# A Mamba-style mixer on one core: cumulated decays loaded as repeated rows in place of TensorE's spreading

## What is computed

```python
proj = einsum('bld,pd->blp', layernorm(x), in_proj_w)      # gate 4096, hbc 6144, dt 64
xBC = silu(causal_conv(hbc, 4 taps))                       # x: 64 heads x 64; B, C: 8 groups x 128
dt_p = softplus(dt + dt_bias); A = -exp(A_log)
state = state * exp(dt_p * A) + dt_p * x * B               # per head, row by row
y = state @ C + x * D
out = (group_norm(y) * norm_weight * silu(gate)) @ out_proj_w
```

## Time and profile before

| | |
|---|---|
| runs | median 1298.97 us (1296.31 to 1299.89), 3 runs |
| profiled execution | 1300.67 us |
| its span, first to last instruction | 1298.9 us |
| TensorE busy | 1230.5 us, 95% |
| VectorE busy | 933.9 us, 72% |
| ScalarE busy | 702.5 us, 54% |
| GpSimd busy | 653.6 us, 50% |

### The profile page before, as it was taken

How to read it: one execution, slowest core, us unless ns; L and a number is a source line. 1 busy time by engine, 2 the same in 40 slices (tenths; PEclk the granted TensorE clock), 3 DMA queues, 4 the chain that set the end, 5 groups by cost and what they waited for, 6 DMA issues and landing times. The chain is left out here.

```text
span 1298.9 us, 22009 instructions
## 1 busy us (share of the span) xinstructions
PE 1230.5 (95%) x6680; PEld 968.9 (75%) x6690; DVE 933.9 (72%) x1735; ACT 702.5 (54%) x1056; POOL 653.6 (50%) x707
## 2 busy tenths in 40 slices
PE   5999999999999999999999999999679999889976
PEld 4777777787778778777778878777557777667754
DVE  5786778669667866966886696688567555479995
ACT  3676676567567666756766675665543333222210
POOL 5057546655655655565465556545653343433330
PEclk9999999999999999999999999999789999889996
DMA  5111021011102101110210110010103322211100
GB/s 178 46 50 34 2 67 34 19 34 49 33 1 66 33 17 33 50 32 1 66 32 17 33 58 24 5 34 2 41 17 115 97 90 83 93 49 48 45 16 25
DMA packets 44233, 57.52 MB, mean 44 GB/s; under 512 B 10117, under 2 KB 21159, under 8 KB 43929
## 3 DMA queue, kind: packets, MB, share of 16 engines
q1 hardware_dynamic: 44185, 56.92, 14.3%
HBM read 49.95 MB, written 6.96 MB: 44 GB/s over the span
## 5 line engine op out<-in xcount | busy, mean ns | idle before, releaser
L722 DVE SCALAR_TENSOR_TENSOR conv<-p_tile,conv_taps,conv 128x511 f32<-128x511 f32 x189 | 141.3, 748 | 51.4 <-ACT conv L583 36.4
L831 DVE TENSOR_TENSOR em<-em,p_gb 128x512 f32<-128x512 f32 x128 | 82.1, 683 | 69.6 <-ACT em L630 69.5
L527 POOL TENSOR_TENSOR squares<-squares 128x256 f32<-128x256 f32 x64 | 48.0, 750 | 132.5 <-ACT squares L656 132.5
L94 PE MATMUL p_tile<-xn_hi,wc_hi 128*128 128x512 f32 x252 | 110.8, 440 | 0.9 <-DVE halo L726 0.9
L656 ACT ACTIVATE squares<-y 128x512 f32<-128x512 f32 x64 | 40.4, 631 | 112.5 <-DVE y L867 111.5
L722 DVE SCALAR_TENSOR_TENSOR conv<-p_gate,conv_taps,conv 128x511 f32<-128x511 f32 (+2 forms) x90 | 67.0, 745 | 46.7 <-ACT conv L583 43.1
L94 PE MATMUL p_tile<-xn_lo,wc_hi 128*128 128x512 f32 x252 | 98.8, 392 | 0.0
L94 PE MATMUL p_d<-wr_hi,zt_hi 128*128 128x512 f32 x236 | 94.0, 398 | 1.5 <-ACT em L630 1.5
L94 PE MATMUL p_d<-wr_lo,zt_hi 128*128 128x512 f32 x236 | 93.1, 394 | 0.0
L495 POOL TENSOR_TENSOR x_w<-xs,head_g 128x512 f32<-128x512 f32 x56 | 58.4, 1043 | 68.7 <-ACT xs L624 63.6
L588 ACT ACTIVATE xbc<-conv 128x512 f32<-128x512 f32 x96 | 60.7, 632 | 59.7 <-DVE conv L730 37.4
(11 more groups left out here) (393 smaller groups left out, 3605.1 us busy)
## 6 DMA issues: line engine op xcount, KB each, us to landing
w_raw<-w SPq DMA_DIRECT2D x108, 256.0 KB, 2.7
q_words<-q SPq DMA_DIRECT2D x33, 256.0 KB, 2.7
h_ring<-h_lo_rows SPq DMA_DIRECT2D x6, 704.0 KB, 4.8
h_lo_rows<-h_rest SPq DMA_DIRECT2D x11, 256.0 KB, 2.1
x_res<-x SPq DMA_DIRECT2D x8, 256.0 KB, 4.1
out<-out_t SPq DMA_DIRECT2D x8, 256.0 KB, 2.0
h_lo_rows<-h_rest SPq DMA_DIRECT2D x11, 128.0 KB, 1.9
gate_second<-w SPq DMA_DIRECT2D x4, 256.0 KB, 5.0
```

The source lines that it names most:

```text
L94: pe.matmul(out, lhs(k)[0], rhs(k)[n], start=(start and k == 0 and n == 0), stop=False)
L722: ve.scalar_tensor_tensor(out=conv[:, s, sh:], in0=p[:, 0:HALF - sh], scalar=conv_w[:, bass.ds(g, 1), j, tap], in1=conv[:, s, sh:], op0=AL ...
L831: ve.tensor_tensor(m, m, gm.unsqueeze(1).broadcast_to([P, HG // 2, P]), ALU.mult)\
```

## The change

- TensorE's decay products go, with `d_lhs`, `d_rhs`, `head_rows`, `load_d` and the bf16 parts. cum and exp(cum) are written to DRAM in fp32 as rows (`cum_rows`, `e_cum_rows`).
- `load_cum` loads the row block of a chunk's 8 heads, 1024 numbers, into all 128 partitions of em (512 KB), two chunks ahead, after s_intra of the buffer's last reader. `load_e_cum` loads each head's row into its 64 channels of e_cum (two DMAs of 128 KB), one chunk ahead, after s_t. VectorE's product with e_cum waits for s_ecl.
- `decay_steps` on ScalarE: for each of 8 heads Relu(cum_s - cum_t), 128x128, in place, with a column of cum_tok as bias, one chunk ahead, before the wait for s_y. Then em = exp(-that). Entries with s > t become 1 and are masked by VectorE's product. The exp of e_cum leaves the chunk loop.
- TensorE's waits for s_e and s_d go; those for s_v, s_res and s_t stay or move.
- Prologue: ScalarE normalizes (`ln_norm`), VectorE makes -mean times rstd of one column; ScalarE and GpSimd split w_dt, GpSimd makes the mask. The conv tiles use the banks p_tile, p_d1, p_in, p_x, p_tile, p_d1; four of them and a gate tile come before the transposes of dt.

The diff, cut (declarations, renumbered waits and removed constants are left out):

```diff
...
+    FIRST_BANK = (p_tile, p_d1, p_in, p_x, p_tile, p_d1)
...
-        def load_d(g, c):
+        def load_cum(g, c):
             n = g * NC + c
-            lhs_row, rhs_row = at(sp, g * PART * HG), at(sp, g * PART)
-            wait(sp, s_d, n - 1)
-            cs = slice(c * P, (c + 1) * P)
-            sp.dma_start(d_lhs[PART:PART + PART * HG, c % 2, :],
-                         parts.rearrange("g k h t -> (g k h) t")[bass.ds(lhs_row, PART * HG), cs])\
-                .then_inc(s_dl[c % 2], 16)
-            sp.dma_start(d_rhs[0:PART, c % 2, :].rearrange("k (h t) -> k h t", h=HG),
-                         parts.rearrange("g k h t -> (g k) h t")[bass.ds(rhs_row, PART), :, cs])\
-                .then_inc(s_dl[c % 2], 16)
+            wait(sp, s_intra, n - 1)
+            row = at(sp, g + c * G)
+            sp.dma_start(em[:, c % 2, :], cum_rows.rearrange("c (g h) t -> (c g) (h t)", g=G)[bass.ds(row, 1), :]
+                         .broadcast_to([P, HG * P])).then_inc(s_dl[c % 2], 16)
+        def load_e_cum(g, c):
+            wait(sp, s_t, g * (NC - 1) + c - 1)
+            row = at(sp, g + c * G)
+            own = e_rows.rearrange("c (g j a) t -> (c g) a j t", g=G, a=2)[bass.ds(row, 1)]
+            for a in range(2):
+                sp.dma_start(by_tile(e_cum[a * HD:(a + 1) * HD, :]),
+                             own[:, a, :, :].broadcast_to([HD, GW // P, P])).then_inc(s_ecl, 16)
...
-        for k in range(PART):
-            wait(sp, dt_ve, 12 + k)
+        for rows, made in ((cum_rows, (ln_st, NC + 3)), (e_rows, (dt_ac, 7))):
+            sp.wait_ge(*made)
             for a in range(2):
-                sp.dma_start(parts[:, k, :, a * HALF:(a + 1) * HALF], t_parts[k][a * H:(a + 1) * H, :])\
-                    .then_inc(s_parts, 16)
-        sp.wait_ge(s_parts, 16 * PART * 2)
-        sp.wait_ge(s_dconst, 80)
-        load_d(0, 0)
-        load_d(0, 1)
+                heads_a = (t_cum if rows is cum_rows else t_ecum)[a * H:(a + 1) * H, :]
+                sp.dma_start(rows[a * CH:(a + 1) * CH].rearrange("c h t -> h c t"),
+                             heads_a.rearrange("h (c t) -> h c t", t=P)).then_inc(s_parts, 16)
+        sp.wait_ge(s_parts, 16 * 4)
+        load_cum(0, 0)
+        sp.wait_ge(dt_tp, 4)
+        sp.wait_ge(dt_ve, 9)
+        load_cum(0, 1)
...
+                if c + 1 < NC:
+                    load_e_cum(g, c + 1)
                 if c + 2 < NC:
-                    load_d(g, c + 2)
+                    load_cum(g, c + 2)
                 elif not last:
-                    load_d(g + 1, c + 2 - NC)
+                    load_cum(g + 1, c + 2 - NC)
...
+        pool.memset(t_mask, 1.0).then_inc(s_split_dt, 1)
+        pool.wait_ge(s_split_dt, 1)
+        pool.memset(t_mask[:, 0:HALF:P], 0.0).then_inc(s_split_dt, 1)
...
+        pool.wait_ge(dt_ac, 1)
+        pool.tensor_tensor(lo_of(WT - 1), w_dt[:], hi_of(WT - 1).bitcast(F32), ALU.subtract).then_inc(s_split_dt, 1)
...
+        def decay_steps(g, c):
+            act.wait_ge(s_dl[c % 2], 16 * (g * (NC // 2) + c // 2 + 1))
+            for h in range(HG):
+                steps = em[:, c % 2, h * P:(h + 1) * P]
+                made = act.activation(steps, steps, ACT.Relu, scale=-1.0, bias=cum_tok[:, c, bass.ds(g * HG + h, 1)])
+            made.then_inc(s_e, 1)
...
-                act.wait_ge(s_d, n + 1)
-                wait(act, s_intra, n - 1)
-                if last and c >= CH:
-                    act.activation(e_cum[:], p_in[:], ACT.Exp).then_inc(s_ec, 1)
-                for k, p in enumerate((p_d0, p_d1)):
-                    act.activation(em[:, c % 2, k * 512:(k + 1) * 512], p[:], ACT.Exp).then_inc(s_e, 1)
-                if c > 0 and not (last and c >= CH):
-                    act.activation(e_cum[:], p_in[:], ACT.Exp).then_inc(s_ec, 1)
+                act.wait_ge(s_e, 3 * n + 1)
+                for k in range(2):
+                    decay = em[:, c % 2, k * 512:(k + 1) * 512]
+                    act.activation(decay, decay, ACT.Exp, scale=-1.0).then_inc(s_e, 1)
...
+                if c < NC - 1:
+                    decay_steps(g, c + 1)
+                elif not last:
+                    decay_steps(g + 1, 0)
...
+        def ln_norm(c):
+            act.wait_ge(ln_var, 3 * c + 3)
+            wait(act, ln_tr, c - 1)
+            act.activation(xnt[:, c % 2, :], x_res[:, c, :], ACT.Identity, bias=mean_var[:, c, 0:1],
+                           scale=rstd[:, c:c + 1]).then_inc(ln_xn, 1)
...
+        for c in range(NC + 1):
+            if c < NC:
+                ln_norm(c)
+            if c > 0:
+                ln_round(c - 1)
+            if c == CH:
+                act.wait_ge(s_const, 16 * 6)
+                act.activation(hi_of(WT - 1), w_dt[:], ACT.Copy).then_inc(dt_ac, 1)
+            if c > CH:
+                w_round(0, c - CH - 1)
...
+        tile_in(0, 0, 0, FIRST_BANK[0])
...
             tile_silu(j, 0, j, 0)
+            if j + 2 < TILES:
+                tile_in(j + 2, 0, j + 2, FIRST_BANK[j + 2])
             if j == 0:
+                gate_silu(0, 0, 0)
+                act.wait_ge(ln_st, NC + 3)
+                act.activation(t_ecum, t_cum, ACT.Exp).then_inc(dt_ac, 1)
+                act.wait_ge(dt_tp, 3)
+                act.activation(by_half(dtw_t), transposed(p_gb), ACT.Exp).then_inc(dt_ac, 1)
+                act.wait_ge(dt_tp, 4)
+                act.activation(by_half(etot_t), transposed(p_gate), ACT.Exp).then_inc(dt_ac, 1)
+            if j == 3:
+                gate_silu(1, 1, 0, p_in)
+            if j == 4:
                 gate_silu(2, 2, 0, p_x)
-            if j + 2 < TILES:
-                tile_in(j + 2, 0, j + 2, (p_tile, p_d1)[j % 2])
         gate_silu(3, 3, 0)
+        act.wait_ge(dt_ve, 11)
+        decay_steps(0, 0)
...
-            if 2 <= c < NC + 2:
-                ve.wait_ge(ln_rs, c)
-                wait(ve, ln_tr, c - 3)
-                ve.tensor_scalar(xnt[:, c % 2, :], x_res[:, c - 2, :], mean_var[:, c - 2, 0:1],
-                                 rstd[:, c - 2:c - 1], ALU.subtract, ALU.mult).then_inc(ln_xn, 1)
+            if 1 <= c <= NC:
+                ve.wait_ge(ln_rs, c + 1)
+                ve.scalar_tensor_tensor(out=mean_var[:, c - 1, 0:1], in0=mean_var[:, c - 1, 0:1], scalar=-1.0,
+                                        in1=rstd[:, c - 1:c], op0=ALU.mult, op1=ALU.mult).then_inc(ln_var, 1)
...
+        tile_taps(0, 0, 0, 0, range(TAPS), FIRST_BANK[0])
...
-        tile_taps(0, 0, 0, 0, range(TAPS), p_tile)
+        tile_taps(1, 0, 1, 0, range(TAPS), FIRST_BANK[1])
         ve.wait_ge(dt_tp, 3)
         ve.tensor_copy(by_half(dt_t), transposed(p_y)).then_inc(dt_ve, 1)
-        for j in range(1, TILES):
-            tile_taps(j, 0, j, 0, range(TAPS), (p_tile, p_d1)[j % 2])
-        ve.wait_ge(dt_ac, 7)
-        ve.wait_ge(dt_ve, 15)
+        ve.tensor_copy(by_half(cum_tok), transposed(p_d0)).then_inc(dt_ve, 1)
+        for j in range(2, TILES):
+            tile_taps(j, 0, j, 0, range(TAPS), FIRST_BANK[j])
...
-                wait(pe, s_tap, TAPS * (j - 1))
+                wait(pe, s_tap, TAPS * (j - 3))
...
-                pe.wait_ge(s_e, 2 * (n + 1))
+                wait(pe, l2_lo, {2: 1}.get(k, 0))
...
-                pe.wait_ge(s_dl[c % 2], 32 * (g * (NC // 2) + c // 2 + 1))
-                if c > 0:
-                    wait(pe, s_t, g * (NC - 1) + c - 1)
-                    for j in range(GW // P):
-                        pe.matmul(p_in[:, j * P:(j + 1) * P], head_rows[:, j, :], d_lhs[:, c % 2, :],
-                                  start=True, stop=True)
-                wait(pe, s_e, 2 * n)
-                wait(pe, s_res, n - 2 if tail and c > CH else n - 1)
-                wait(pe, s_v, n - 1)
                 if first:
                     pe.wait_ge(s_tap, TILES * TAPS)
-                for k in rows_in(last, c - 1):
-                    pe.wait_ge(l2_lo, k + 1)
-                for k, p in enumerate((p_d0, p_d1)):
-                    mm = pe.matmul(p[:], d_lhs[:, c % 2, :], d_rhs[:, c % 2, k * 512:(k + 1) * 512],
-                                   start=True, stop=True)
-                mm.then_inc(s_d, 1)
...
-                    pe.wait_ge(s_e, 2 * (n + 1))
+                    wait(pe, s_v, n - 1)
...
-                    pe.wait_ge(s_ec, g * (NC - 1) + c)
+                    wait(pe, s_t, g * (NC - 1) + c - 1)
...
+        conv_tile(0, 0, 0, 0, FIRST_BANK[0])
+        pe.wait_ge(dt_ve, 2)
+        for j in range(1, CH):
+            conv_tile(j, 0, j, 0, FIRST_BANK[j])
         gate_product(0, 0, 0)
-        gate_product(0, 1, 0, p_in)
+        pe.wait_ge(dt_ve, 9)
+        for src, dst in ((t_dt, p_y), (t_rem, p_gb), (t_cum, p_d0)):
+            for b in range(CH):
+                mm = pe.transpose(dst[:, b * P:(b + 1) * P], src[:, b * P:(b + 1) * P], ident[:])
+            mm.then_inc(dt_tp, 1)
+        for j in range(CH, TILES):
+            conv_tile(j, 0, j, 0, FIRST_BANK[j])
+            if j == CH:
```

(14 more changed lines are left out.)

126 lines of the change are left out of this document (32 added, 94 removed).

## The result

The changed kernel takes 1276.23 us, median of runs between 1275.21 and 1276.79; the kernel before, timed beside it, 1297.72. The ratio is 0.983, 95% interval 0.981 to 0.985: 21.5 us faster, a gain, but about half of the 44 forecast. So of the 22.5 us that are missing in the medians 18.5 are missing in the traces too, and those have places.

The account below looks back on a forecast made before the run. TensorE, busy all of a group's round, was taken as the bound. Columns 37.7, less 3 of waits, plus prologue 5.5 and tail 4 made 44 us, so a median of 1255; range 1241 to 1276.

Parts of the forecast that it names:

- rivals 1 and 3: ScalarE takes over as the bound, 1270 to 1286, 17%; SyncE's order makes weights late in chunk 0, 1276, 5%.
- TensorE's columns: Decay products gone from the mixer's chunks: 0.67 us saved per chunk, 0.44 in chunk 0, 37.7 us in all.
- A wait of about 0.1 us: Next chunk's conv tile waits for the gate's Silu in p_tile, in four chunks of a group: 3 us lost.
- With eight register offsets on top I allow 4: ScalarE's eight Relu steps per chunk: 2.6 us taken, 0.31 apart, upper bound 4 us with register offsets.
- Hidden: In chunk 0 the Relu steps make Square and xs 2.4 us later, without TensorE waiting for x_w.
- Prologue: Before the mixer: dt products start 4 us sooner, 1.5 us of bank waits go; 5.5 us saved, bounds 1 and 8.
- Tail: Last group's chunks 5 to 7: waits for xn_lo and e_cum go, x_w late next; 4 us saved, bounds 0 and 12.3.
- Transfers: Each chunk's 512 KB row block lands in 4 us, bounds 2.7 and 7, and is hidden, as are the out weights.
- The second: The ends give more, prologue 8 and tail 12 us, with no loss: 57.7 us saved, 1241; 10%.
- fourth: Slower: the 128 copies of one row land late and the first Relu waits for s_dl; 1396, 4%.
- fifth: The change doesn't do what it says, as TensorE's columns were hidden; 1295, 3%.

Follow-up runs that it names:

- tuned: both, but in the last four chunks of the last group the product of C and the state keeps its old place; 1257.26 us, ratio 0.967.
- both: Changed kernel with the product of C and the state ahead of the conv tile and ScalarE's loop written out; 1258.47 us, ratio 0.967.
- wide_relu: tuned with a chunk's eight Relu steps made one of 128x1024 with a single bias column (decays not the reference's); 1251.95 us, ratio 0.963.
- inter_first: Changed kernel with TensorE's product of C and the state moved ahead of the same chunk's conv tile; 1266.67 us, ratio 0.976.
- scalar_unrolled: Changed kernel with ScalarE's loop over the six middle groups written out, other engines keeping theirs; 1268.12 us, ratio 0.976.
- before_long_body: Kernel before with nine unread one-column Relu steps per chunk on ScalarE, each with its own register; 1314.97 us, ratio 1.013.
- best: tuned with chunk 0's Relu steps behind z_round in groups 1 to 6 only; 1256.56 us, ratio 0.967.
- no_register: Changed kernel with each Relu taking its bias column at a fixed address, without register offsets (wrong columns in seven groups); 1269.51 us, ratio 0.977.
- before_padded: Kernel before with eight unread one-column Relu steps per chunk on ScalarE, sharing registers; 1310.98 us, ratio 1.008.

## Why the prediction came out half right

The median, 1276.23, is the far end of the stated range, 1241 to 1276. The range was drawn that far for halves of rivals 1 and 3, and neither made this time: that the time and the end of the range meet is luck, and the gain is half of the forecast.

Chunks 0 to 58, forecast and measured (us saved), each term from the stages above (tuned has the 798.8 of both, so the terms close by construction; the evidence for each is its own run):

| term | forecast | measured | from |
|---|---|---|---|
| columns and what goes with them | 37.7 | 40.9 | before against wide_relu |
| Relu steps in the queue | 0 | -5.6 | tuned against wide_relu |
| the bank p_tile | -3 | -9.1 | after against inter_first |
| return of ScalarE's loop | 0 | -6.1 | after against scalar_unrolled |
| the two together, beyond their sum | 0 | -2.8 | after against both |
| sum | 34.7 | 17.3 | |

**TensorE's columns**: right, and a little more. Chunks 3, 4 and 7 save 0.64 us where 0.67 were forecast, chunk 0 saves 0.44 as forecast. Most of the 3.2 us above is chunk 1, which saves 0.86 in wide_relu, and 2.3 in group 0. There the out product of the kernel before waits 1.5 us until the exp of em has read p_d0; with em out of PSUM this is gone, a gain that the prediction had not seen.

**"A wait of about 0.1 us"** for the Silu in p_tile is the first step that failed; it is the 3 us of the sum. The place was right, the size and the cause were wrong. I set the Silu's end, 601.35, against 601.32, when TensorE would want the bank, and took the Relu steps for what could delay it. They don't: in chunk 5 the Silu starts when its own product ends. From that end to the next weight load in the bank pass 0.04 + 0.60 us and another 0.2 after the Silu, 0.85 in all (584.53 to 585.38), and between them stand only the transposes and B C^T, since the product is the last thing ahead of them. I had left out the 0.2. It costs 0.32 us in chunks 5 and 6, and 0.4 to 0.5 in chunks 1 and 2; only ahead of chunk 2 is the Silu itself late behind the steps (the 2.4 us of TensorE's waits). The decay products had covered this with nothing in the trace that says so.

**"With eight register offsets on top I allow 4"**, as ScalarE's time: there the offsets cost nil (389 ns with and without), and steps 0.29 apart, 2.44 us for eight, met the 0.31 and 2.6. The Trainium skill's 387 ns and 2.4 us (ScalarE: Activation LUTs, What ACT_TABLE_LOAD costs), which the prediction set beside its own, come still closer. What I left out is the length of the program, and this is the second step that failed, by omission: ScalarE's loop body grew from 218 to 342 instructions, and each of five returns cost 3.5 us of ScalarE and 1.2 of TensorE, 6.1 in all and 8.9 once the bank is mended. No part of the prediction counted instructions, nor did a rival.

**"Hidden"**, chunk 0's delay of 2.4 us, is the third: at least 5.6 us, with 1.1 us of Relu a chunk still there. Of these 1.29 are chunk 0 of group 0, where the prologue's term had taken 0.5. For the others I had followed xs, and not Square and z_round, behind which the out product of chunk 1 waits. In group 1:

```profile
179.54 0.60 ACT L628 ACTIVATE gate_second<-p_tile 128x512 f32<-128x512 f32 x1 [2.42 <-PE p_tile L95]
180.03 2.44 ACT L605 ACTIVATE em<-em,cum_tok 128x128 f32<-128x128 f32 x8
182.38 0.62 ACT L669 ACTIVATE squares<-y 128x512 f32<-128x512 f32 x1
182.90 0.58 ACT L598 ACTIVATE zt_hi<-p_y 128x512 fp32r<-128x512 f32 x1
```

y was there at 179.77; without the steps zt_hi would end 2.4 us sooner than its 183.48. In the kernel before, Square starts right behind that Silu, after no idle time: the 1.75 us a chunk was a mean, and in chunk 0 it is nil in seven of eight groups.

**Prologue** (5.5): 4.1. The dt products start at 19.27, 2.75 us sooner and not 4: seven of VectorE's eight one-column steps (L939) took 142 to 160 ns, as taken (150), but the last, right ahead of the dt products, took 1215, 1.1 us more. Why is open. What follows them shrank by 1.4, as forecast (1.5). **Tail** (4): 4.0 between the two traces, but most of it is the granted clock: a hit by luck, see below. **Transfers**: 512 KB land in 4.0 us as taken, and hide.

**The rivals.** The first, ScalarE as the bound, would have given 1270 to 1286 and the time fell there, but its condition did not come true: the steps were 0.29 apart, and after chunks 4 and 5 the bank p_tile comes free late with the Silu on time. A part of its mechanism did occur, at two places of a group: ahead of chunk 2 the Silu is late behind the steps, and in chunk 1 zt_hi is, the 5.6 us above. The third has the very time, 1276, and nothing of its mechanism: no round starts with out weights that are late, and a third of the traffic less changes no chunk once the loop is gone. A time that fits a rival is not yet that rival. The second, fourth and fifth did not occur.

**The tail.** Chunks 59 to 62 by themselves: before, before_long_body, after, both, best (length, busy us by engine, then granted clock, DMA share, GB/s):

```profile
895.00:952.62 57.62, 45.29 (x258) 33.90 (x257) 36.18 (x78) 28.47 (x46) 34.78 (x44) 0.85 0.09 24
913.13:967.39 54.26, 42.73 (x258) 32.48 (x257) 36.15 (x78) 33.59 (x76) 34.43 (x44) 0.91 0.10 25
873.62:927.27 53.65, 39.52 (x234) 30.69 (x232) 36.91 (x79) 34.12 (x70) 33.90 (x44) 0.90 0.31 87
856.20:914.37 58.17, 43.88 (x234) 33.28 (x232) 37.33 (x79) 34.46 (x71) 33.81 (x44) 0.79 0.31 81
854.33:907.67 53.34, 39.04 (x235) 30.31 (x233) 37.19 (x79) 34.46 (x71) 33.84 (x44) 0.90 0.32 89
```

both and best have the same matmuls and the same three long waits (7.4, 3.1, 3.1 us). TensorE is busy 4.84 us longer in both, and the stretch is 4.83 longer: it did the same work at a lower granted clock, 0.79 for 0.90, a mix of the two levels with more of 1.2 GHz. In both kernels the clock first fell within the wait of 7.4 us, the longest of the stretch. All fourteen traces fall in line: 52.8 to 54.3 us at 0.90 or 0.91, 56.6 to 57.6 at 0.85, 58.2 to 58.4 at 0.79 or 0.80. And it is not a matter of the kernel alone: the executions of both go from 1255.41 us (mean clock 0.980) to 1261.10 (0.974), and those of the kernel before from 1296.31 to 1303.55.

So the 4.0 us of the tail are mostly no gain. The decay products are still there in before_long_body, and at a clock like the changed kernel's its tail takes 54.26, 0.6 us more than the 53.65. The forecast added 4 us for the two waits that go, for xn_lo and e_cum, 12.3 us. They went, but in the changed kernel TensorE waits there for GpSimd's x_w instead (from 850 to 985 us):

```profile
PE p_x L1122 <- POOL x_w L495: 13.5, 3, 7.2
```

The prediction had named x_w as the next thing late, but only 0.3 us later than before; it took the place of the waits in full. The prologue's 4.1 and the middle's 17.3 alone make 21.4 of the 21.5 us of the medians. These are single traces of each kernel: the size is a hint, not a measurement, and what decides the clock of an execution is open. It is as large as what the last experiments changed, so those are read from chunks 0 to 58.

## What to carry to other kernels

Before an instruction is taken out of a full engine, ask what it was covering: follow each bank or buffer that the next instruction needs back to its last reader, and count the time from the end of the work that feeds that reader. When a step adds instructions to a loop on any engine, count the instructions of the whole body, those that make addresses or only wait too, and look at the first instruction of each round. And take the time of each stage chunk by chunk: two causes that no wait in the trace names, and one time that fitted the wrong rival, came apart only there. Where a stage has waits, look at its granted clock too before two traces of it are compared.

## What the runs showed of the hardware

Whether ScalarE stands still at each return of its loop went with the length of the loop body. ScalarE's instructions in a round by the records of the trace (register instructions and separate waits counted), instruction packets of its queue in the run, time from the branch to the next instruction, and idle time ahead of the first work of a round, for five returns:

| kernel | body | packets | branch to next, us | idle us |
|---|---|---|---|---|
| before | 218 | 23 | 0.3 | 0.0 |
| no_register | 278 | 24 | 0.3 | 0.0 |
| before_padded | 290 | 24 | 0.3 | 0.0 |
| after | 342 | 50 | 3.8 to 4.4 | 17.5 |
| before_long_body | 356 | 51 | 2.4 to 2.6 | 9.6 |

The separate waits belong in the count: with the loop written out the queue fetched eight packets of 8 KB in the 550 us from 253 to 803, five rounds of 204 recorded instructions with the waits: 1020 in 64 KB, 64 bytes each.

The Trainium skill (Runtime: NRT & Kernel Launch, Instruction fetch mechanics) says that most engines hold their instructions in two blocks of 256, and that a taken branch to a place outside of them stops the engine until the block has come. An estimate from that page's figure: a body of up to 257 instructions always fits in two blocks, and one of up to 512 may or may not, by where it starts. The traces agree as far as they go: 278 and 290 did not stop, 342 and 356 did. Where a body starts was not varied, so the limit between 290 and 342 holds for these kernels. That the stop of ScalarE's work is 1.9 to 3.8 us is from the runs alone.

And in PSUM: from the end of a product to the start of the next product's weight load in the same bank, with one 128x512 Silu between, 0.85 us passed (584.53 to 585.38 in the changed kernel).
